# Up, down and output products split into halves and placed by a build-time table; lead 23 with the order of a unit's heads tied to its parity

## The reference

```python
def fp4_quant_dequant(x):            # blocks of 16 along the last axis
    scale = max(max(abs(block)) / 6, 1e-12)
    q = GRID[searchsorted(MID, abs(x / scale))] * sign(x / scale) * scale
xn = layernorm(x)
scores = einsum("bhqd,bhkd->bhqk", q, k) / sqrt(8) + slope[h] * (k_pos - q_pos)
attn_out = softmax(scores) @ v @ Wo + bo
gate, y = fp4_linear(xn, w_gate), fp4_linear(xn, w_up)      # 128 -> 352
ffn_out = fp4_linear(silu(gate) * y, w_down)                # 352 -> 128
return x + attn_out + ffn_out
```

## Time and profile before

| | |
|---|---|
| median of 3 runs | 901.35 us (899.79 to 916.80) |
| the profiled execution's own time | 894.07 us |
| span of its instructions | 892.3 us |
| TensorE busy, share of the span | 772.9 us, 87% |
| VectorE | 741.1 us, 83% |
| ScalarE | 633.0 us, 71% |
| GpSimd | 349.3 us, 39% |
| mean granted TensorE clock | 0.962 |

### The profile page before, as it was taken

How to read it: one execution, slowest core, us unless ns; L and a number is a source line. 1 busy time by engine, 2 the same in 40 slices (tenths; PEclk the granted TensorE clock), 3 DMA queues, 4 the chain that set the end, 5 groups by cost and what they waited for, 6 DMA issues and landing times.

```text
span 892.3 us, 13552 instructions
## 1 busy us (share of the span) xinstructions
PE 772.9 (87%) x4939; PEld 225.7 (25%) x4939; DVE 741.1 (83%) x878; ACT 633.0 (71%) x1262; POOL 349.3 (39%) x271
## 2 busy tenths in 40 slices
PE   3279989898989989897989989898989898979896
PEld 2012223221223323231323323222213231313222
DVE  7898898889888888978898888989897989898920
ACT  4106878777777878776877778777777687767775
POOL 7272172624226373715053553615152505141320
PEclk9557999999999999999999999999999999999999
DMA  5900020131001020320102020310102000000000
GB/s 156 256 13 2 1 72 3 52 92 36 3 13 37 13 72 2 101 44 1 37 2 49 13 73 1 107 37 1 37 2 49 13 3 1 2 1 2 2 1 24
DMA packets 32826, 31.83 MB, mean 36 GB/s; under 512 B 4344, under 2 KB 26552, under 8 KB 32760
## 3 DMA queue, kind: packets, MB, share of 16 engines
q1 hardware_dynamic: 32760, 30.96, 12.8%
HBM read 15.91 MB, written 15.04 MB: 35 GB/s over the span
## 4 chain that ended last, share of the span: by engine, by line
PE 58%; DVE 27%; ACT 8%; issue 4%; POOL 2%; DMA 1%; SPq 0%; ACTq 0%; DVEq 0%; POOLq 0%
PE low L966 22%; DVE neg_max L811 19%; PE mx L936 18%; ACT probs L630 6%; PE low L955 5%; PE mx L1005 3%; PE mx L989 3%; PE low L983 2%; DVE am L784 1%; DVE mb L804 1%; PE low L922 1%; ACT pv_s L667 1%; PE low L997 1%; DVE hid L826 1%; DVE inv L798 1%
## 5 line engine op out<-in xcount | busy, mean ns | idle before, releaser
L811 DVE TENSOR_REDUCE neg_max<-mx 128x1 f32<-128x1024 f32 x512 | 611.6, 1221 | 91.6 <-PE mx L936 80.2
L630 ACT ACTIVATE probs<-low 128x512 f32<-128x512 f32 x1024 | 552.0, 603 | 182.1 <-PE low L955 180.4
L936 PE MATMUL mx<-k_op,q_op 51*128 51x512 bf16 x1024 | 318.5, 398 | 55.9 <-DVE neg_max L811 33.4
L955 PE MATMUL low<-q_op,k_op 53*128 53x512 bf16 x1024 | 329.0, 389 | 8.0 <-ACT probs L630 2.5
L966 PE MATMUL low<-probs,v_op 128*32 128x512 f32 x2048 | 277.4, 614 | 7.1 <-ACT pv_s L667 5.9
L551 POOL TENSOR_SCALAR tanh_s<-tanh_s 128x704 f32<-128x704 f32 x16 | 31.7, 1982 | 313.7 <-ACT gate_s L681 313.7
L936 PEld LDWEIGHTS mx<-k_op,q_op 51*128 51x128 bf16 x1024 | 62.6, 95 | 358.5 <-DVE neg_max L811 197.2
L955 PEld LDWEIGHTS low<-q_op,k_op 53*128 53x128 bf16 x1024 | 68.5, 94 | 76.5 <-ACT probs L630 63.8
L489 POOL TENSOR_SCALAR mb<-mb 128x960 f32<-128x960 f32 (+2 forms) x17 | 58.8, 3456 | 39.6 <-DVE mb L804 37.9
L966 PEld LDWEIGHTS low<-probs,v_op 128*32 128x32 f32 x2048 | 40.5, 108 | 89.9 <-issue 46.1
L477 POOL TENSOR_TENSOR zb<-hid,inv 128x704 f32<-128x704 f32 x16 | 22.2, 1387 | 97.7 <-DVEq L799 97.7
(11 more groups left out here) (120 smaller groups left out, 522.3 us busy)
## 6 DMA issues: line engine op xcount, KB each, us to landing
q_op<-q_rows SPq DMA_DIRECT2D x32, 192.0 KB, 3.8
k_op<-k_rows SPq DMA_DIRECT2D x32, 192.0 KB, 4.7
q_rows<-qp SPq DMA_DIRECT2D x8, 384.0 KB, 2.6
k_rows<-kp SPq DMA_DIRECT2D x8, 384.0 KB, 3.2
x_s<-in_L_attn_inputs_dram SPq DMA_DIRECT2D x8, 256.0 KB, 3.7
q_rows<-qp SPq DMA_DIRECT2D x8, 256.0 KB, 3.1
k_rows<-kp SPq DMA_DIRECT2D x8, 256.0 KB, 3.1
out_dram<-o_s SPq DMA_DIRECT2D x8, 256.0 KB, 2.3
```

The lines of the kernel that those rows point to most:

```text
L630: nc.scalar.activation(probs[U % 3][:, 2 * g + x, :], bank("exp", U, j), ACT.Exp).then_inc(st_free, 1)
L811: nc.vector.tensor_reduce(to, slot("max", pos)[:], AX.X, ALU.max, negate=True).then_inc(mx_free, 1)
L936: ins = nc.tensor.matmul(slot("max", pos)[:, 512 * kh:512 * kh + 512], q, k, start=True, stop=True)
L955: nc.tensor.matmul(bank("exp", U, j), k_op[quad][r, g, kt * P:(kt + 1) * P], q_op[quad][r, g, half * HALF:(half + 1) * HALF], start=True, ...
```

## The change

`LEAD` is 23 instead of 22, and `HEAD` is computed from the lead's parity, so that a chunk still runs beside scores of the other parity. `up`, `down` and `wo` become two jobs each, `(…, 0)` and `(…, 1)`, with a ring slot and an emptying instruction for each half. `extras(U)` gives way to a table `AT` that `plan()` fills: each job takes the first free unit from a wished one on, with one place in the **middle** of a unit (where all jobs stood before) for `gate`, `q`, `k`, `v`, the weights' transposes and `bvo`, and one at its **end**, behind the value product, for all others. ACT copies `pv_s` after the first exponential of its unit instead of after the second. DVE finds the block maxima right behind the second half of `up` and the inverse one chunk after the scales. POOL normalizes, splits and rounds at units that follow the table.

```diff
-LEAD = 22
+LEAD = 23
...
-HEAD = ((1, 0), (1, 1), (0, 0), (0, 1))
+FFN_FIRST, FFN_STEP = 4, 15
+MIDDLE = ("gate", "q", "k", "v", "gT", "uT", "dT", "bvo")
+HEAD = tuple((x, g) for x in ((LEAD + 1) % 2, LEAD % 2) for g in range(2))
+def norm_unit(b):
+    return 1 if b == 1 else 60 * b - 59
+def parts_unit(g):
+    return 60 * (g // 2 - 1) + 16 + 15 * (g % 2)
+def plan():
+    at, busy = {}, set()
+    def put(first, *job):
+        place = job[0] in MIDDLE
+        while (first, place) in busy:
+            first += 1
+        busy.add((first, place))
+        at[job] = first
+        return first
+    for U, job in enumerate(("bvo", "gT", "uT", "dT")):
+        put(U, job)
+    for m in range(HALVES):
+        if m >= LEAD // 16:
+            put(turn_unit(m), "turn", m)
+        put(KT * (m + 1) + 2, "pvT", m)
+    x_at = put(FFN_FIRST, "xT", 0)
+    for p in range(NP):
+        U = put(x_at + 1, "gate", p, 0)
+        U = put(U + 1, "gate", p, 1)
+        U = put(U + 2, "up", p, 0)
+        up = put(U + 1, "up", p, 1)
+        if p + 1 < NP:
+            x_at = put(max(FFN_FIRST + FFN_STEP * (p + 1), up + 7), "xT", p + 1)
+        U = put(up + 7, "hT", p, 0)
+        U = put(U + 1, "hT", p, 1)
+        U = put(U + 1, "down", p, 0)
+        put(U + 1, "down", p, 1)
...
+    for hb in range(2 * B):
+        U = put(at["pvT", hb // 2 * 8 + 6 + hb % 2] + 1, "ctxT", hb)
+        for i in range(2):
+            U = put(max(U, at["down", 2 * hb + 1, 1]) + 1, "wo", hb, i)
+    return at
...
-                for j in range(2):
+                for j in range(4):
                     exponential(U, j)
...
+                    if j == 0 and U % KT == 1 and KT < U <= NU + 1:
+                        m = U // KT - 1
+                        act.wait_ge(pv_done, U - 1)
...
+                        nc.scalar.copy(pv_s[:], pv).then_inc(pv_kept, 1)
+                    for job in middle(U) if j == 1 else ():
+                        job_on_scalar(job)
+                for job in end(U):
+                    job_on_scalar(job)
...
+                    half = slice(t * I, (t + 1) * I)
+                    mark(nc.vector.scalar_tensor_tensor(hid[:, half], gate_s[:, half], 0.5, slot("up", p, t)[:, 0:I],
+                                                        ALU.mult, ALU.mult))
+                    settle()
                     dve.sem_inc(mx_free, 1)
+                    if t == 1:
+                        block_maxima(p + 1)
...
+                    if 0 < U <= NU and i == 1:
+                        value_product(U - 1)
+                    for job in middle(U) if i == 0 else ():
                         job_on_array(job)
-                if 0 < U <= NU:
-                    value_product(U - 1)
+                for job in end(U):
+                    job_on_array(job)
```

More of the change, by code:

```diff
@@ L63 @@
 MAX_IN = 16 * 2
[L72 removed]
+LEAD = 23
 CHUNKS = 2 * B * QUADS * UNITS
 HALVES = 2 * B * QUADS
[L77 to L82 removed]
+FFN_FIRST, FFN_STEP = 4, 15
+MIDDLE = ("gate", "q", "k", "v", "gT", "uT", "dT", "bvo")
+IN_DVE_RING = ("up", "down", "pvT", "wo", "bvo")
 def turn_unit(m):
@@ L124 @@
-IN_DVE_RING = ("up", "down", "pvT", "wo", "bvo")
+HEAD = tuple((x, g) for x in ((LEAD + 1) % 2, LEAD % 2) for g in range(2))
[30 more added lines that the diff above has]
+        put(U + 1, "down", p, 1)
+    for b in range(1, B):
+        for g in (2 * b, 2 * b + 1):
+            U = norm_unit(b) + 1 + 8 * (g % 2)
+            for name in ("xnT", "q", "k"):
+                U = put(U + 1, name, g)
+            assert U < parts_unit(g)
+            put(max(U, QUADS * UNITS * (b - 1) + 2) + 1, "v", g)
+    for hb in range(2 * B):
[3 more added lines that the diff above has]
+    return at
@@ L127, in rings, with middle, end @@
+AT = plan()
+JOBS = {}
+for _job, _unit in AT.items():
+    JOBS.setdefault(_unit, []).append(_job)
+def middle(U):
+    return [job for job in JOBS.get(U, ()) if job[0] in MIDDLE]
+def end(U):
+    return [job for job in JOBS.get(U, ()) if job[0] not in MIDDLE]
 def rings():
@@ L143, in rings, with to_ring @@
             to_act("turn", 0)
-    for U in range(NU + KT):
+    def to_ring(job):
+        (to_dve if job[0] in IN_DVE_RING else to_act)(*job)
+    for U in range(NU + 2 * KT):
         for i in range(2):
@@ L985, in job_on_array @@
                 elif kind == "up":
-                    free_slot("up", p)
+                    t = job[2]
+                    free_slot("up", p, t)
                     pe.wait_ge(st_free, max(ST["xT", p], ST["uT",]) + 1)
-                    for t in range(2):
-                        ins = nc.tensor.matmul(slot("up", p)[:, 512 * t:512 * t + I], xqT[:, t * P:(t + 1) * P], uT_s[:],
-                                               start=True, stop=True)
-                    ins.then_inc(mx_full, 1)
+                    nc.tensor.matmul(slot("up", p, t)[:, 0:I], xqT[:, t * P:(t + 1) * P], uT_s[:],
+                                     start=True, stop=True).then_inc(mx_full, 1)
                 elif kind == "hT":
@@ L1000, in job_on_array @@
                 elif kind == "down":
[L1001 to L1006 removed]
+                    t = job[2]
+                    free_slot("down", p, t)
+                    pe.wait_ge(st_free, max(ST["hT", p, t], ST["dT",]) + 1)
+                    for c, (_, n) in enumerate(IC):
+                        ins = nc.tensor.matmul(slot("down", p, t)[:, 0:P], hqT[t][0:n, c * P:(c + 1) * P],
+                                               dT_s[0:n, c * P:(c + 1) * P], start=(c == 0), stop=(c == 2))
                     ins.then_inc(mx_full, 1)
```

225 lines of the change are left out of this document (98 added, 127 removed).

## The result

The changed kernel takes 909.30 us (median of 4 runs, 908.26 to 913.36) against 900.57 us of the kernel before on the same chip (4 runs): ratio 1.0117, with an interval of 1.0081 to 1.0152. It is 1.2% slower, a small loss but clear of the interval, and 21 us above the 888 forecast. One run of the kernel before, 916.80 us, was slow and is left out of the ratio. The profiled execution took 909.44 us, its span is 907.4, its mean granted clock 0.962, as before.

The account below looks back on a forecast made before the run. Two almost equal bounds: the PE-ACT loop, 2.46 us a unit, and DVE, 2.41. Job terms sum to 170.8 us surplus against 185.8; with the ends, net -13.3 gives 880.8, plus 7.3 from profile to median: 888 us, eight in ten 873 to 904.

Parts of the forecast that it names:

- rounding on DVE: Units from the second half of `up` on: DVE never idle, 2.1 us late a pair, 15 pairs, 31.5 us.
- maxima late: Halves behind a gather, where the block maxima return too late: 0 to 6 us, 3 taken.
- clock: Four places of 3.4 us at granted clock 0.50: 0 to 6.6 us may stay lost, 2 taken.
- POOL: Rounding on POOL ahead of `hT` and next `xT`: free, by 1 us; about 1 us of waiting expected in pair 9.
- rival 2: Nothing gained: 111 DVE-ring end jobs cost 0.1 us more each, POOL's margin fails in some pairs; 902 us, 18%.
- `xT` wait for POOL: Sign that the forecast is wrong: `hT` or `xT` wait for POOL's rounding, which was forecast free by 1 us.
- `up`: 1.38, halves 0.69: `up` at unit ends, between value product and scores: 32 halves of 0.69 us, 22.1 against 16.5 before.
- Jobs in those units come free: -7: Units where DVE is late with the rounding: `xnT`, `q`, `k` and `wo` there cost nothing, 7 us off.
- the bound of 2.46 us: Length of a unit without a job; 256 make 629.8 us, and the loop's time above that is the surplus.
- rival 3: Block maxima's round trip, now behind the value product, comes too late for first scores of a half: 923 us, 6%.
- rival 4: Scores and chunks no longer run beside each other, if the parity were wrong: an estimated 200 us more, 1%.
- Rival 1: The loop is all that was wrong: surrounding units absorb DVE's lateness, no clock fall stays; 870 us, 20%.

Follow-up runs that it names:

- experiment 1: Changed kernel with POOL's normalization of the fourth sequence at unit 120 instead of 121, ahead of pair 8's rounding: 904.43 us, ratio 1.0022 to the kernel before.
- experiment 2: experiment 1 with POOL's `three_parts` of groups 6 and 7 at units 138 and 154 instead of 136 and 151: 898.17 us, ratio 0.9961 to the kernel before.
- experiment 5: experiment 1 with `up` and `down`, still halved, in the middle of their units: median 902.37 us, ratio 1.0059 to the kernel before.
- experiment 3: experiment 1 with `up` and `down` whole again in the middle, maxima and scales placed as before: 882.12 us, ratio 0.9775 to the kernel before.
- experiment 8: Kernel before with lead 23, `HEAD` for its parity and `turn` at the end of its unit: 889.16 us, ratio 0.9905.
- experiment 7: experiment 3 with `pvT` in the middle of its unit: 897.65 us, ratio 1.0004 to the kernel before.
- experiment 10: Kernel before, no table, with lead 23, `HEAD` order, `turn` and `pvT` at unit ends, `pv_s` copied after the first exponential: 891.06 us, ratio 0.9920.
- experiment 6: experiment 3 with `up` and `down`, still whole, moved to the end of their units: 899.95 us, ratio 1.0014 to the kernel before.
- experiment 11: experiment 3 with `pv_s` copied after the second exponential again: 888.70 us, ratio 0.9898 to the kernel before.
- experiment 9: Kernel before with only `pvT` moved to the end of its unit, lead 22: 899.80 us, ratio 1.0049.
- experiment 4: Kernel before with only the copy `pv_s` moved behind the first exponential of its unit: 903.18 us, ratio 0.9999.

## Why the prediction was wrong

The surplus of the loop, forecast and measured (us; a term is its number of units by the cost in units where it stands alone):

| step | forecast | after |
|---|---|---|
| `xnT`(6) behind the normalization, units 123 and 124 | 0 | 8.4 above experiment 1 |
| pair 9 behind `three_parts`, units 158 and 159 | 1 | 4.1 above the same units of experiment 2 |
| `up`, first half | 0.69 | 1.02, 11 times, and 1.07 and 1.15: +4.5 |
| rounding on DVE with the jobs in it (the five units from the second half of `up` on, less the forecast's prices of their jobs) | 24.5 | about 30 |
| `wo` of units 60, 140, 188 | 0.51 each | 2.8, 2.0, 2.3: +5.6 |
| `down`, a half | 0.765 | 0.87 |
| `pvT` | 0.48 | 0.60 |
| `hT`, `xT`, `pv_s`, `turn` | 0.46, 0.35, 0.20, 0.18 | 0.48, 0.37, 0.16, 0.03 to 0.3 |
| maxima late | 3 | 0.3, in one half |
| clock | 2 | 17.1 us at half clock in four places (13.7 before); the loss is inside the rows above |
| ahead of the first unit | +1.2 | +3.9, 2.7 of it the cast of the last section |

The first five rows sum to about 27 us against the 26.1 by which the surplus was missed; the rows below it take the small remainder in both directions. The 21 us between the medians are less than that by luck: the forecast carried over the 7.3 us by which one profiled execution lay under its median, and for the changed kernel there is no such distance (909.44 and 909.30). From profile to profile the miss is 909.44 - 880.8 = 28.6 us.

**The step that failed is "POOL"**, and first by what it left out. It priced the rounding against `hT` and the next `xT` ("free, by 1 us") and named pair 9, but not the normalization, although the change moves all three of POOL's jobs relative to each other. A queue that runs in order has to be read as a list: who waits for each entry, and what stands ahead of it. Experiment 1 shows the mechanism (8.4 us in two units), and experiments 1 and 2 the price of POOL's order, 11 to 14 us together. It is the second half of rival 2 ("POOL's margin of 1 us fails"), at a greater price, and one of the prediction's own signs of being wrong ("`xT` wait for POOL"). The 1 us taken for pair 9 failed as well: `xT` waits 2.60 in the changed kernel, and the units behind it run with DVE late and at low clock; where it doesn't wait, in experiment 1, the same late rounding costs through the cast of `neg_parts`.

**The sizes of the end jobs.** "`up`: 1.38, halves 0.69" divided a duration by two. A half takes 0.79 by itself, in units 54 and 244 for instance, with no wait of PE behind it; `down` 0.87 for 0.765 and `pvT` 0.60 for 0.48 (units 99 and 98) are PE's own time in the same way, and not the wait for DVE of rival 2's first half. The first half of `up` costs 1.02 where it shares its unit with `neg_parts`. Unit 116, PE and DVE:

```profile
447.61 0.86 PE L1043 MATMUL mx<-uT_s,xqT 128*128 128x352 f32 x2
448.63 0.39 PE L990 MATMUL mx<-k_op,q_op 51*128 51x512 bf16 x1 [0.16 <-DVE neg_max L859]
```

```profile
447.26 0.18 DVE L865 TENSOR_TENSOR neg_parts<-neg_max,neg_parts 128x16 bf16<-128x16 f32 x1
447.35 1.22 DVE L859 TENSOR_REDUCE neg_max<-mx 128x1 f32<-128x1024 f32 x1
448.50 0.52 DVE L876 SCALAR_TENSOR_TENSOR hid<-gate_s,mx 128x352 f32<-128x352 f32 x1
```

The two instructions of `neg_parts` stand ahead of the unit's second reduction, and the chunk behind `up` waits for that reduction, which ends at 448.57; `hid` comes only after it. Experiment 5 shows that halves cost in the middle too, so it isn't only the place.

**The halves of `wo` in units 60, 140 and 188** cost little by themselves: 0.64 in units 203 and 252. In these three the cast of `neg_parts` waits for POOL (2.02, 1.25 and 1.22 us, in unit 188 the subtraction another 0.54, all against 0.17), and PE stands 2.05, 1.28 and 1.62 us behind it. The prediction has no term for such a meeting.

**"Jobs in those units come free: -7"** fell for `wo`: behind the second half of `up` they aren't hidden but lengthen the line in front of DVE, 2.1 to 2.5 us in units 87, 151 and 199.

**What held**: the bound of 2.46 us, `hT`, `xT`, the place of `turn` (no PE wait of note is left for `neg_parts`), `pv_s` at the end of the range given, `pvT` without the wait behind it, the statement that `down` and `up` get dearer when moved to the end, and the maxima's way back: PE waits for the reads in one half, 0.3 us. So rival 3 is out; rival 4 too, since scores and chunks still start together. Rival 1 is out as well (its sum had a slip: half of 31.5 and 5 are 21 and not 18, so 867 us). Of the Trainium skill's rule on small instructions, cited in the prediction, only this can be said: half of `hid` takes 0.52 us for 352 columns where the whole took 0.89, so 0.15 of fixed time, as the row-based price had it.

**A match by luck.** Experiment 3 keeps every term that held and drops the two that the prediction itself called dearer. Its surplus of 171.4 us is almost the forecast's 170.8, but the forecast was for the halves: by the prediction's own prices of the whole jobs (18.4 for 24.5 and 16.5 for 22.1) experiment 3 should have stood at 159. The change as a whole was two good moves (`turn` with lead 23, about 1% alone in experiment 8; `pvT` with `hT` and `xT` out of the middle, which makes the early copy pay) and three bad ones (POOL's order, the halves, `up` and `down` behind the value product), the last two of which cost as much alone as together.

**What stays open**: how the 19 us of experiment 5 divide between the split and the places that then change, and how much of each median hangs on falls of the clock. The profiles show between one and nine of them in the loop, in places that differ from kernel to kernel. The count of PE's waits doesn't order them: experiment 7 has 74 waits of over half a microsecond and two falls, experiment 10 has 62 and eight. If half of the time at low clock is lost at most (an estimate), experiment 3, with 3.4 us of it, owes up to 3.4 us of its distance to experiments 6 and 7 (10.2 each) to the clock, and up to 8.5 of its distance to experiment 1 (20.5). A run that changes the clock alone wasn't made.

## What to carry to other kernels

Before an order is changed, write each in-order queue that the change touches as a list, the helper engine's too, with who waits for each entry: the most expensive wait here was on the engine that is idle for over 60% of the time. A job is charged by the place in the loop where it stands, and places interact: the same copy, moved by one exponential, was worth 0 in one arrangement and 6.6 us in the other, so a measured gain belongs to its surroundings. Halving a job doesn't halve its cost: half an `up` took 0.79 us where the whole took 1.38, and 1.02 where it met a late reduction.

## What the runs showed of the hardware

**A small DVE instruction can last until POOL's running one ends.** The cast of `neg_parts`, 16 columns, takes 0.17 us. In unit 60 of the changed kernel:

```profile
263.14 2.23 POOL L534 TENSOR_TENSOR zb<-zb,mb 128x960 f32<-128x960 f32 x1
263.38 2.02 DVE L864 CAST neg_parts<-neg_max 128x16 bf16<-128x16 f32 x1
...
266.80 0.39 PE L990 MATMUL mx<-k_op,q_op 51*128 51x512 bf16 x1 [2.05 <-DVE neg_max L859]
```

It ends within 0.04 us of the POOL instruction, and so do all that are long. Those of over 0.5 us are 9 of 64 `neg_parts` instructions before (10.2 us in all beyond 0.17 each), 7 after (7.3 us), 8 in experiment 3, 13 in experiment 10. It depends on what POOL runs: in the changed kernel all 14 that begin beside a TENSOR_TENSOR of POOL's last over 0.25 us, and none of the 6 beside a TENSOR_SCALAR; over all 13 profiles it is 168 of 184 and 12 of 61. The 512 reductions, which read PSUM, keep their mean of 1.22 us and none is longer than 1.23. PE then stands in line: 2.05 us here. The Trainium skill (SBUF — State Buffer, "SBUF: two separate sides") says that VectorE's second port pair is shared with GpSimd as an exclusive lock, held for a whole instruction, and needed by VectorE for a 2-port mode or for two operands in SBUF; by that rule the casts and the subtraction would wait and the reductions from PSUM would not, and the traces agree; that most of those beside a TENSOR_SCALAR don't wait is not explained by it. In sum the waits are no longer after the change than before (7.3 us against 10.2), but they fall elsewhere: in units 60, 140 and 188 they are most of what the forecast missed there.

**One such meeting ahead of the loop is worth 2.7 us.** In the same instruction of the prologue, in the changed kernel and then in experiment 3:

```profile
12.79 0.94 POOL L491 MEMSET k_op<- 128x1024 f32 x1
13.23 3.73 DVE L807 CAST probs<-probs 16x1024 bf16<-16x1024 f32 x1
13.68 0.94 POOL L492 MEMSET q_op<- 128x1024 f32 x1
14.58 0.94 POOL L491 MEMSET k_op<- 128x1024 f32 x1
15.47 0.94 POOL L492 MEMSET q_op<- 128x1024 f32 x1
```

```profile
13.23 1.04 DVE L805 CAST probs<-probs 16x1024 bf16<-16x1024 f32 x1
13.69 1.49 POOL L490 MEMSET q_op<- 128x1024 f32 x1
```

Here the cast ends only behind four POOL instructions in a row. Of the 13 profiled executions, eight have the cast at 3.73 us and five at 1.04 or 1.05 (before, experiments 3, 5, 10 and 11). First units start at 70.6 to 72.3 us with the long cast where the lead is 23 and at 68.2 to 68.7 with the short one (experiment 5's execution apart). That is most of the +3.9 in the table above, and some 3 us of the distance between the profiles of experiment 3 and of experiments 6 and 7. The instructions there are the same in all kernels, so it is not the change that made the cast long; whether one and the same kernel shows both is not known, since each has one profile.

**The low clock's size.** Most falls in the loop last 3.41 us, some 6.83; experiment 9 has one of 10.24 and experiment 4 one of 40.96. The granted clock in them is 0.50, level 1.2 GHz. PE's instructions in them take nearly twice their time (value product 1.94 for 1.06). What PE did before: in the changed kernel the four falls come behind waits of 2.05 us, of 0.65 and 0.62, in the middle of the one of 6.28, and behind one of 2.60; in all profiles there is a wait of at least 0.6 us shortly ahead, but most waits of that size are followed by no fall.
